# Masked cross attention: TensorE computes a step's scores ahead of all four heads' transposes

## The reference, cut to what matters

```python
def _L1_xattn_ref(q, encoder_k, encoder_v, encoder_attention_mask, wo_w, wo_b):
    ...
    qh = _split_heads(q)
    kh = _split_heads(encoder_k)
    vh = _split_heads(encoder_v)
    scores = jnp.einsum('bhqd,bhkd->bhqk', qh, kh) + encoder_attention_mask
    weights = jax.nn.softmax(scores, axis=-1)
    ctx = jnp.einsum('bhqk,bhkd->bhqd', weights, vh)
    ctx = ctx.transpose(0, 2, 1, 3).reshape(q.shape[0], q.shape[1], -1)
    return jax.nn.relu(ctx @ wo_w.T + wo_b)
...
x = x + _L1_xattn_ref(_layernorm(x, axis=-1), ctx_1024, ctx_1024, mask_Bx1xSxS2_ff0, L1_xattn_wo_w, L1_xattn_wo_b)
```

## Time and profile before

| | |
|---|---|
| time before, median of 3 runs | 1381.54 us (1379.87 to 1383.92) |
| the profiled execution, its own time | 1385.54 us |
| its span | 1383.8 us |
| TensorE busy | 1238.0 us, 89% of the span |
| VectorE busy | 682.8 us, 49% |
| ScalarE busy | 530.4 us, 38% |
| the masked cross attention in the span | 698.9 to 884.7 us |

### The profile page before, as it was taken

One profiled execution on the slowest core, in us unless ns is written; L12 is line 12 of the kernel. 1 busy time (PEld: TensorE's weight loads), 2 busy tenths in 40 slices (PEclk: granted clock), 3 DMA queues, 4 the chain that ended last, 5 costly groups with the idle time before them and its releaser, 6 DMA issues. The chain is left out here.

```text
span 1383.8 us, 22965 instructions
## 1 busy us (share of the span) xinstructions
PE 1238.0 (89%) x9706; PEld 990.1 (72%) x9706; DVE 682.8 (49%) x1129; ACT 530.4 (38%) x793; POOL 206.8 (15%) x169
## 2 busy tenths in 40 slices
PE   5899999999999999397748998597669999999998
PEld 4688888887888886137315666376459999999997
DVE  3554535454654334325157774205265666656663
ACT  3432333234232321003127887213244444444442
POOL 1044334343344324000000000000000000000000
PEclk9999999999999999786759999898879999999999
DMA  6110101000000100440042320320035444445440
GB/s 260 62 47 1 46 3 45 32 17 32 17 17 1 62 1 2 179 179 0 0 183 93 123 93 32 143 101 1 4 135 200 183 183 182 185 188 193 193 180 16
DMA packets 27294, 124.97 MB, mean 90 GB/s; under 512 B 2315, under 2 KB 2459, under 8 KB 16709
## 3 DMA queue, kind: packets, MB, share of 16 engines
q1 hardware_dynamic: 27046, 123.56, 23.6%
q0 software_dynamic: 160, 0.13, 0.0%
HBM read 123.16 MB, written 0.52 MB: 89 GB/s over the span
## 5 line engine op out<-in xcount | busy, mean ns | idle before, releaser
L646 POOL TENSOR_TENSOR norm_both<-norm_both,prob 128x512 f32<-128x512 f32 x120 | 156.8, 1307 | 146.6 <-DVE prob L455 139.1
L57 PE MATMUL mo_h_ps<-mo_x_hi,mo_w_hi 128*128 128x256 f32 x512 | 145.6, 284 | 5.9 <-DVE mo_w_lo L1487 5.9
L58 PE MATMUL mo_h_ps<-mo_x_lo,mo_w_hi 128*128 128x256 f32 x512 | 145.5, 284 | 0.0
L59 PE MATMUL mo_h_ps<-mo_x_hi,mo_w_lo 128*128 128x256 f32 x512 | 145.4, 284 | 0.0
L578 ACT ACTIVATE prob<-u_ps 128x512 f32<-128x512 f32 x128 | 66.1, 605 | 175.1 <-PE u_ps L732 175.1
L438 DVE TENSOR_TENSOR turned<-k_ps,tabs 128x512 f32<-128x512 f32 x32 | 22.1, 690 | 198.3 <-PE k_ps L59 198.3
L1493 DVE TENSOR_TENSOR mo_w_lo<-w_raw,mo_w_hi 128x2048 fp32r<-128x2048 f32 x32 | 73.3, 2292 | 74.5 <-ACT mo_w_hi L1452 74.5
L57 PE MATMUL k_ps<-ctx_hi,wk_hi 128*128 128x512 f32 x256 | 103.5, 404 | 3.7 <-DVE wk_lo L426 3.7
L57 PE MATMUL u_ps<-wv_hi,ctx_hi 128*128 128x512 f32 x256 | 102.3, 400 | 3.1 <-ACT prob L578 1.9
L57 PEld LDWEIGHTS mo_h_ps<-mo_x_hi,mo_w_hi 128*128 128x128 f32 x512 | 98.8, 193 | 8.7 <-DVE mo_w_lo L1487 7.5
L58 PE MATMUL k_ps<-ctx_lo,wk_hi 128*128 128x512 f32 x256 | 100.8, 394 | 0.0
(11 more groups left out here) (238 smaller groups left out, 2353.1 us busy)
## 6 DMA issues: line engine op xcount, KB each, us to landing
w_raw<-in_w SPq DMA_DIRECT2D x64, 1024.0 KB, 6.4
ctx_raw<-in_ctx_rows SPq DMA_DIRECT2D x8, 1024.0 KB, 5.6
x_k<-in_ctx_T SPq DMA_DIRECT2D x8, 1024.0 KB, 5.0
x_val<-in_ctx_heads SPq DMA_DIRECT2D x8, 1024.0 KB, 4.9
tabs<-in_rot_tabs SPq DMA_DIRECT2D x8, 512.0 KB, 3.3
vals<-in_wq_rows SPq DMA_DIRECT2D x4, 512.0 KB, 6.7
ctx_raw<-in_wo SPq DMA_DIRECT2D x1, 2048.0 KB
x_mask<-in_mask SPq DMA_DIRECT2D x2, 1024.0 KB, 15.7
```

Of the source, the lines that this page charges most:

```text
L57: pe.matmul(out, w_hi, x_hi, start=start, stop=False)
L58: pe.matmul(out, w_hi, x_lo, start=False, stop=False)
L59: return pe.matmul(out, w_lo, x_hi, start=False, stop=stop)
L646: ins = pool.tensor_tensor(to, to, src, ALU.add)
```

## The change

TensorE's loop now puts `scores(t)` first in a step, and all four `turn(q, a)` behind it in one run. Before, heads 0 and 1 were transposed ahead of the scores, and heads 2 and 3 behind them. Nothing else is touched: the other engines' programs, every wait and every buffer are the same (line numbers behind the edit fall by three).

```diff
             for t in range(NST + LAG + 1):
                 q, w = t - LAG, t - LAG - 1
-                if 0 <= q < NST:
-                    turn(q, 0)
-                    turn(q, 1)
                 if t < NST:
                     scores(t)
                 if 0 <= q < NST:
-                    turn(q, 2)
-                    turn(q, 3)
+                    for a in range(4):
+                        turn(q, a)
                 if w >= 0:
                     weigh(w)
```

## The result

The changed kernel takes 1403.72 us (median of 4 runs, 1402.81 to 1409.94), the kernel before 1381.15 us (median of 4, 1379.87 to 1383.92). The ratio is 1.017, with a 95% interval of 1.0137 to 1.0203: slower by 22.6 us. The forecast was 1404.5 us, with a range of 1398.5 to 1411.

The account below looks back on a forecast made before the run. TensorE's work plus waits for exponentials bound the old loop; VectorE's ring would bound the new one. 24 steps of 5.43 us, plus start and end, gave 23.0 us delay: 1381.5 + 23.0 = 1404.5 us, range 1398.5 to 1411.

Parts of the forecast that it names:

- The ring: In the loop, scores, transposes, VectorE's copy and masks close before the next scores: 5.43 us a step, against 4.66.
- five edges: Scores to transposes 1.07, to copy 1.13, to first mask 0.64, four masks 2.45, last read to next scores 0.14 us.
- The gain that was given up: Scores behind the weighing cover TensorE's 0.86 us wait for exponentials, by itself worth two waits in four steps.
- the faster rival: Exponentials' wait at every second step's first transposes decides; scores fill it, saving 11 us: 1370.5 us, chance 0.03.
- TensorE's slack: TensorE's own work is 4.85 us a step, leaving it idle some 0.6 to 0.9 us in each step.
- The start: Scores of t = 6 start unchanged at 727.62; those of t = 7 at 734.6, or 735.0 if the clock is low.
- cold: Step 7 at low clock: ring of 7.33 us, 1.9 more; total delay 24.2 us, against 21.9 warm.
- the middle: Total delay taken as 23.0 us, between 21.9 with a warm step 7 and 24.2 with a cold one.
- The clock: TensorE's granted clock stays at 1.00 in the loop from t = 8; its fall for most steps had chance 0.06.
- the new gaps: TensorE's idle gaps of 0.6 to 0.9 us a step, set against a clock fall after a 2.55 us wait.
- what the forecast cites from the Trainium skill: Full clock does not engage for transposes; by that rule steps with sixteen transposes between idle gaps drop to low clock.

Follow-up runs that it names:

- Experiments 1: The changed kernel with VectorE copying head 0 instead of head 1, and ScalarE copying heads 1, 2 and 3: 1393.43 us, kernel before on the same chip 1382.89.
- experiment 3: The changed kernel with one 128x512 VectorE memset added in each step behind the copy of head 1: 1416.50 us, kernel before on the same chip 1382.89.
- experiment 4: The kernel before with one 128x512 VectorE memset added in each step behind the copy of head 1: 1382.25 us, kernel before on the same chip 1382.89.
- experiment 6: The changed kernel with LAG 7 instead of 6: 1405.43 us, kernel before on the same chip 1381.39.
- Experiment 5: The kernel before with LAG 7 instead of 6, transposes and weighing one step later: 1370.14 us, ratio 0.9918 to before.
- experiment 2: The changed kernel with VectorE doing each step's masks ahead of its copy of head 1: 1437.94 us, kernel before on the same chip 1382.89.
- experiment 9: The changed kernel with two 128x512 VectorE memsets added behind the copy of head 1: 1436.30 us, kernel before on the same chip 1383.85.
- experiment 8: The changed kernel with VectorE's masks ahead of its copy, plus nine zero matmuls ahead of head 3's transposes in three of four steps: 1438.91 us.

## Why the prediction was right

**The ring.** Forecast 5.43 us a step, allowed 5.30 to 5.55; measured 5.40, and 5.49 once in four, in the steps with `top`. In a plain step each of its five edges came within 0.02 us of the forecast's. In the steps of 5.49 the fifth edge, from VectorE's last read to the next scores, is 0.23 us in place of 0.14 (757.30 to 757.53). `top` stands behind the last mask there, and the next scores are the first of a group and also wait for new keys; which of the two costs the 0.09 us was not tried. Experiments 1 and 3 changed one edge each and moved the step by that edge; experiment 4 showed that the same work outside the ring is free.

**The gain that was given up.** The forecast said that the wait for exponentials would be covered, and counted nothing for it. The waits show none for them up to t = 32, and experiment 6 shows that more room for them brings nothing to the step. Experiment 5 puts a price on it where TensorE is the bound: 11.4 us of the stage, net of what one more step of lag costs, near the 11 us that the faster rival was given.

**TensorE's slack.** 0.6 to 0.9 us a step were forecast. The rows say 0.79 in plain steps and 0.37 in those with `widen`, counted from modelled ends, so the second lies below the range. By starts it is 741.24 - 739.37 = 1.87, less 1.01 for the weighing: 0.86. With `widen` it is 0.3 to 0.4 less. (The forecast's sum for TensorE, 1.07 + 2.46 + 1.0 + 0.3, is 4.83 and not 4.85; nothing hangs on it.)

**The start.** The scores of t = 7 were to follow those of t = 6 by 7.0 to 7.4 us, and the next step to be 5.43 us if warm and 7.33 if cold; I took the middle. Measured on TensorE:

```profile
721.65 2.09 PE L1122 MATMUL x_s_ps<-x_k,norm_both 32*128 32x512 f32 x8 [2.66 <-DVE x_tops L1253]
...
726.32 0.66 PE L1140 MATMUL x_t_ps<-ident,x_sc 128*128 128x128 f32 x4 [0.18 <-DVE x_pT L1238]
728.77 2.09 PE L1122 MATMUL x_s_ps<-x_k,norm_both 32*128 32x512 f32 x8 [1.80 <-DVE x_tops L1253]
...
735.84 1.14 PE L1122 MATMUL x_s_ps<-x_k,norm_both 32*128 32x512 f32 x8 [0.88 <-DVE x_tops L1253]
```

The two are 7.12 and 7.07 us. Step 7 was cold (at half clock), and it had become cold again, since the last four transposes of step 6 had run at the full clock (0.66 us) and a wait of 1.80 us followed. From the scores of t = 6 to the transposes of t = 32 the forecast had 23.0 us more than before; the trace has 866.14 - 721.65 = 144.49 against 121.03, which is 23.5. The cold step added 0.7 to the middle that I had taken (7.07 against 6.38), and the start and the 23 steps at 5.42 in the mean took 0.3 away. That the total came so near is partly luck: the forecast did not see the second fall of the clock, and its middle between a warm and a cold step hid that.

**The clock.** It stayed at 1.00 in the steady loop, as forecast. The stage's own start was the exception. The reason given was weaker than it looked: I had set the new gaps against a fall behind 2.55 us, while falls turned up behind 1.80 us in this very kernel and behind 1.47 us in experiment 2. Nor was that fall the nearest one, as I had called it. The trace of the kernel before has later falls, one of them at a wait of 2.28 us that ends at 560.61, and near its start it has one at a wait of 1.88 us:

```profile
64.41 0.39 PE L59 MATMUL k_ps<-ctx_hi,wk_lo 128*128 128x512 f32 x1
...
68.67 0.66 PE L57 MATMUL u_ps<-wv_hi,ctx_hi 128*128 128x512 f32 x1 [1.88 <-ACT prob L578]
```

The microsecond behind it as a stretch (the last three figures are PEclk, DMA share and GB/s):

```profile
69.00:70.00 1.00, 1.00 (x4) 0.71 (x4) 0.85 (x2) 0.99 (x3) 0.00 (x0) 0.50 0.00 0
```

The gaps of 0.6 to 0.9 us were still shorter than any of these, so the forecast held, but with less room than its text gives. In the changed kernel sixteen transposes in a row, 0.25 us of waiting among them, ran at the full clock in every step from t = 8 on. For this case that is the opposite of what the forecast cites from the Trainium skill, TensorE: Matmul & The Clock Gate, section "Part 4: PE-mode transpose". Scores and weighing stand between these runs of transposes in every step; what transposes alone would do no run here shows.

## What to carry to other kernels

Before moving work ahead on one engine, follow the ring through the other engines' fixed orders: an engine that is half idle can still set the pace when an unrelated copy stands ahead of what the next step waits for. Sum the ring edge by edge from start-to-start distances in the old trace; here that gave the plain step to 0.03 us. Where a wait is for results made just in time, one more step of lag between producer and consumer can remove it without changing any order.

## What the runs showed of the hardware

TensorE's clock fell behind shorter waits than the 1.88 us of the kernel before. In loops of the same kind of work it stayed at 1.00 with a wait of 0.79 us in a step of 5.40 and with 1.33 us in one of 5.94 (experiment 3). With 1.47 us in a step of 6.14 it fell in some steps and not in others, and with 1.87 us in one of 6.48 likewise, each time for some 3 us. In experiment 9 the scores of two steps that followed waits of 1.86 and 1.87 us took 1.14 and 1.87 us. What decides whether it falls was not tried. Adding useless matmuls inside the wait of 1.47 us kept the clock and made the stage 14.0 us shorter (241.7 to 227.7). Of the times that is one execution each, on two chips: 1437.94 against 1425.34 us.

A plain float32 matmul of 128 columns took 0.22 us at the full clock and shows as two records (nine of them, 18 records, in 2.01 us from the first one's start to the next transposes' start, in experiment 8). A transpose of the same size shows as one record and took 0.13 us (eight in 1.02 us). I had reckoned the matmul at the transpose's 0.13.
